# Expert passes cut at multiples of 128 of the running row count, summed into 64 on-chip slots and scattered from there without gaps

## The reference, cut to what matters

```python
# x: 4096 tokens x 128; E = 32 experts, K = 4, inner width I = 96
scores = sigmoid(x @ gate_w.T)
_, topk_ids = top_k(scores + e_bias, K)
topk_w = take_along_axis(scores, topk_ids); topk_w /= sum(topk_w)
combine = zeros(T, E).at[arange(T), topk_ids].add(topk_w)
a = silu(x @ w1[e]) * (x @ w3[e]) * combine[:, e]      # for every expert e
out = sum over e of a @ w2[e]
x = x + gb * out
```

## Time and profile before

| | us |
|---|---|
| median of 3 runs (730.47, 730.84, 735.51) | 730.84 |
| the profiled execution | 729.48 |
| its span, first to last instruction | 727.0 |
| PE busy | 489.9 (67%) |
| DVE busy | 442.6 (61%) |
| POOL busy | 420.3 (58%) |
| ACT busy | 278.1 (38%) |

### The profile page before, as it was taken

The page is one execution under the profiler, slowest core; times in us unless marked ns, Lnnn a source line. Parts: engine busy times, 40 slices in busy tenths (PEclk is TensorE's granted clock), DMA queues, the critical chain, the costliest instruction groups (busy, mean ns, idle before and its releaser), DMA issues.

```text
span 727.0 us, 15153 instructions
## 1 busy us (share of the span) xinstructions
PE 489.9 (67%) x4424; PEld 381.2 (52%) x4425; DVE 442.6 (61%) x1317; ACT 278.1 (38%) x579; POOL 420.3 (58%) x636
## 2 busy tenths in 40 slices
PE   2568888888887767766666623168768767667157
PEld 0335555555555555655445522067767766567136
DVE  5876888888888754777787787035344343433127
ACT  0256777877877634332433322012222222112000
POOL 5565666666665000477766777607777777677710
PEclk9868999999999999787788755579998899989569
DMA  7993000000060050011111111135334443341178
GB/s 217 293 263 104 0 0 1 0 0 0 0 232 4 1 174 1 28 59 50 57 53 53 54 57 58 57 103 139 104 103 119 115 114 102 98 120 52 51 282 310
DMA packets 65243, 65.94 MB, mean 91 GB/s; under 512 B 8896, under 2 KB 56224, under 8 KB 65200
## 3 DMA queue, kind: packets, MB, share of 16 engines
q1 hardware_dynamic: 47472, 41.28, 19.5%
q0 software_dynamic: 9216, 19.94, 8.1%
q10 hardware_dynamic: 8512, 4.20, 2.0%
HBM read 40.86 MB, written 27.67 MB: 94 GB/s over the span
## 4 chain that ended last, share of the span: by engine, by line
issue 25%; POOL 22%; DVE 20%; PE 19%; ACT 6%; DMA 4%; DVEq 2%; POOLq 1%; SPq 1%; ACTq 0%
POOL ys L630 16%; DVE L L1238 6%; PE PS L996 4%; POOL xs L617 4%; PE PS L881 2%; PE PS L1155 2%; PE PS L1008 2%; POOL QKR L515 1%; ACT YT L684 1%; PE PS L1019 1%; PE PS L856 1%; DMA srep<-in_scale 1%; PE PS L904 1%; PE PS L884 1%; DVE XH L1201 1%
## 5 line engine op out<-in xcount | busy, mean ns | idle before, releaser
L617 POOL DMA_INDIRECT xs<-QKT,posi x128 | 124.8, 975 | 109.3 <-issue 98.3
L1238 DVE TENSOR_TENSOR L<-PS,BIAS 128x768 f32<-128x768 f32 x128 | 116.6, 953 | 39.4 <-PE PS L884 33.7
L677 ACT ACTIVATE PR<-L 128x768 f32<-128x768 f32 x128 | 105.9, 842 | 60.9 <-DVE L L1238 58.7
L630 POOL DMA_INDIRECT ys<-hid,yidx x80 | 76.6, 958 | 45.7 <-issue 25.6
L1086 PE MATMUL PS<-BIAS,V 128*128 x320 | 68.0, 361 | 49.1 <-DVE V L1594 48.8
L630 POOL DMA_INDIRECT ys<-YT,yidx x80 | 76.6, 957 | 24.4 <-issue 23.2
L1086 PEld LDWEIGHTS PS<-BIAS,V 128*128 128x128 f32 x320 | 56.2, 205 | 55.5 <-issue 55.5
L791 ACT ACTIVATE L<-PS 128x384 f32<-128x384 f32 x40 | 19.6, 491 | 162.4 <-PE PS L1086 162.4
L881 PE MATMUL PS<-QKT 32*128 32x256 f32 x512 | 47.3, 439 | 27.2 <-DVE L L1238 25.7
L996 PE MATMUL PS<-YT,w1s 128*128 128x256 f32 x128 | 42.2, 487 | 15.8 <-ACT YT L741 15.8
L1608 DVE TENSOR_TENSOR hid<-PS,tag 128x512 f32<-128x512 f32 x20 | 13.8, 692 | 60.1 <-DMA ys<-hid,yidx 60.1
(11 more groups left out here) (247 smaller groups left out, 1121.4 us busy)
## 6 DMA issues: line engine op xcount, KB each, us to landing
PR<-xs SPq DMA_DIRECT2D x160, 72.0 KB
BIAS<-ys SPq DMA_DIRECT2D x12, 512.0 KB, 7.8
modb<-mod_rows SPq DMA_DIRECT2D x1, 4096.0 KB, 14.3
dist_rep<-dist_row SPq DMA_DIRECT2D x4, 768.0 KB, 7.1
xs<-pad_row SPq DMA_DIRECT2D x1, 2376.0 KB, 19.3
X<-in_x ACTq DMA_DIRECT2D x4, 512.0 KB, 6.9
BIAS<-dist_rep SPq DMA_DIRECT2D x4, 512.0 KB, 9.0
xs<-QKT,posi POOLq DMA_INDIRECT x128, 2.3
```

The source lines that it names most:

```text
L617: pool.indirect_dma_start(out=xs, out_offset=bass.IndirectOffsetOnAxis(ap=posi[j][:, t * TOPK + k:t * TOPK + k + 1], axis=0), in_=ROWS[j][ ...
L630: pool.indirect_dma_start(out=ys, out_offset=bass.IndirectOffsetOnAxis(ap=yidx[par][:, j:j + 1], axis=0), in_=yo[par][:, j * P:(j + 1) * P ...
L677: act.activation(PR[u % 4][:, :], L[u % 2][:, :], ACT.Exp).then_inc(s["exp_done"], 1)
L1238: return dve.tensor_tensor(L[u % 2][:, :].rearrange("p (j w) -> p j w", j=2), PS[:, at:at + 2, 0:HW], BIAS[:, u, :].rearrange("p (j w) -> ...
```

## The change

An expert's rows are still contiguous in its own region of `xs`. Now the rows of all experts, laid end to end, are also cut into 128 **slots** of 128 rows, at multiples of 128 of the running count. A pass is the part of one slot that belongs to one expert: it reads the 128 rows of `xs` that stand where the slot stands for that expert, which may begin before the expert's first row or run over its last. There it meets pad rows with weight 0 and place 0. The results of all passes of a slot are added, so each slot ends up full of real rows. For the counts given above that makes 159 passes; 160 are run, as before.

- **xs.** Pad rows are wanted in front of each region's first row (the 128 rows at the end of the region before it), and behind each expert's last row. The second kind depends on the count: SyncE waits for `pad_ready`, loads the 32 row numbers from `pads` and issues 32 DMAs of 128 rows; the loads of `xg` then wait for `pad_done` besides `scat`. GpSimd's wait for `zero_done` ahead of its first scatter goes.
- **Tables.** DVE computes the slot of each pass and, for each group of 4 slots, the number of passes after which the group is full (`tv` columns 4 to 6, `treg` rows 4 to 6). `skip`, `twice` and `slot_no` go.
- **Slots.** 64 slots lie side by side in `YQ`, a tile of 8,704 columns that takes the place of `Y` and `QKT`. There are 128 slots, so each place lives twice (`LIVES`). ScalarE clears four places of `YQ` and of `yidx` per step, two steps ahead (`clear`, 32 in all); for a second life it first waits on `yst` until the scatters of the first have landed.
- **VectorE.** `y_evac` loads the 4 slot numbers, then for each pass does one fused multiply and add of [128 x 128] from PSUM into the slot and one add of [128 x 1] into `yidx`. Before each it waits for the pass before it on its own semaphore. `y_ev` now counts passes, not steps. The wait for the scatters (`yst`) is no longer here.
- **ScalarE.** The copy of the transposed rows to `xgT` moves here from VectorE (L828 of the changed kernel). Its 40 steps are written out instead of looped.
- **GpSimd.** 128 scatters in groups of 4. Ahead of each group it loads the count of passes from `treg` and waits for `y_ev` to reach it.

```diff
+            sp.wait_ge(s["zero_done"], 32)
+            sp.wait_ge(s["pad_ready"], 1)
+            for g in range(NE // 8):
+                for row in load_many(mybir.EngineType.SP, pads, g * 8, DUMMY):
+                    sp.dma_start(xs[bass.ds(row, P), :], pad_row[:, :]).then_inc(s["pad_done"], 16)
...
             for i in range(GROUP):
                 sp.wait_ge(s[f"scat{i}"], 16 * NT * TOPK // GROUP)
+            sp.wait_ge(s["pad_done"], 16 * NE)
...
-            def y_rows(i, par):
-                pool.wait_ge(s["y_ev"], i + 1 + 2)
-                settle(pool)
-                for j in range(XG):
-                    pool.indirect_dma_start(
-                        out=ys, out_offset=bass.IndirectOffsetOnAxis(ap=yidx[par][:, j:j + 1], axis=0),
-                        in_=yo[par][:, j * P:(j + 1) * P], in_offset=None).then_inc(s[f"yst{par}"], 16)
-
-            with pool.Fori(0, XSTEPS // 2) as two:
-                y_rows(two * 2, 0)
-                y_rows(two * 2 + 1, 1)
+            def y_rows(life):
+                for half in range(2):
+                    groups = SLOTS // YGROUP // 2
+                    for q in range(groups):
+                        m = life * (2 * groups) + half * groups + q
+                        ends_at = pool.value_load(passes_of[:, bass.ds(m, 1)], min_val=1, max_val=XG * (XSTEPS + 2))
+                        pool.wait_ge(s["y_ev"], ends_at)
+                        settle(pool)
+                        for j in range(YGROUP):
+                            n = (half * groups + q) * YGROUP + j
+                            pool.indirect_dma_start(
+                                out=ys, out_offset=bass.IndirectOffsetOnAxis(ap=yidx[:, n:n + 1], axis=0),
+                                in_=YQ[:, n * D:(n + 1) * D], in_offset=None).then_inc(s[f"yst{n // 16}"], 16)
...
+            def rows_ev(i, par):
+                act.wait_ge(s["xt_pe"], i + 1)
+                act.activation(xgT[par], bank(par), ACT.Copy).then_inc(s["xg_ev"], 1)
+
+            def clear(n):
+
+                if n < SLOTS // XG * LIVES:
+                    m = n * XG % SLOTS
+                    if n == NT // XG:
+                        for j in range(GROUP):
+                            act.wait_ge(s[f"scat{j}"], 16 * NT * TOPK // GROUP)
+                    if n >= SLOTS // XG and m % 16 == 0:
+                        act.wait_ge(s[f"yst{m // 16}"], 16 * 16)
+                    act.activation(YQ[:, m * D:(m + XG) * D], zero[:, :].to_broadcast([P, XG * D]), ACT.Copy)
+                    act.activation(yidx[:, m:m + XG].bitcast(F32), zero[:, :].to_broadcast([P, XG]), ACT.Copy
+                                   ).then_inc(s["yz"], 1)
...
-            def y_evac(i, par, buf, turns=None):
+            def y_evac(i, par, buf):
+                slots = load_many(mybir.EngineType.DVE, slots_of, i * XG, SLOTS, XG)
                 dve.wait_ge(s["y_pe"], i + 1 + 2)
-                if turns is not None:
-                    dve.wait_ge(s[f"yst{par}"], turns * (16 * XG))
-                dve.tensor_tensor(yo[par].rearrange("p (j d) -> p j d", j=XG),
-                                  bank(6 + par).rearrange("p (j d) -> p j d", j=XG),
-                                  tag[buf][:, :, 0:1].to_broadcast([P, XG, D]), ALU.mult)
-                dve.tensor_tensor(yidx[par][:, :], tag[buf][:, :, 1], twice[:, bass.ds(i * XG, XG)], ALU.max
-                                  ).then_inc(s["y_ev"], 1)
+                dve.wait_ge(s["yz"], i + 1)
+                for k in range(XG):
+                    dve.wait_ge(s["y_ev"], i * XG + (2 * XG + k))
+                    settle(dve)
+                    to = YQ[:, bass.ds(slots[k] * D, D)]
+                    dve.scalar_tensor_tensor(to, bank(6 + par, D, k * D), tag[buf][:, k, 0:1], to, ALU.mult, ALU.add)
+                    at_ = yidx[:, bass.ds(slots[k], 1)]
+                    dve.tensor_tensor(at_, at_, tag[buf][:, k, 1:2], ALU.add).then_inc(s["y_ev"], 1)
```

More of the change, by code:

```diff
@@ L47 @@
 XG = 4
+SLOTS = 64
+LIVES = YROWS // (SLOTS * P)
+YGROUP = 4
 XSTEPS = XTILES // XG
@@ L193, in build @@
         place_no = sb("place_no", [P, NT * TOPK])
-        pad_no = sb("pad_no", [P, 1])
+        group_no = sb("group_no", [P, 2])
         cnt = sb("cnt", [P, NE])
-        cnti = sb("cnti", [P, NE], I32)
-        ntile = sb("ntile", [P, NE])
+        pads = sb("pads", [1, NE], I32)
+        ends = sb("ends", [P, NE])
+        endi = sb("endi", [P, 2, NE], I32)
+        edge = sb("edge", [P, 2, NE])
+        part = sb("part", [P, NE])
+        upto = sb("upto", [P, NE])
+        lead = sb("lead", [P, NE])
         tend = sb("tend", [P, NE])
@@ L800, in _, with step @@
             act.sem_inc(s["at_act"], 2)
[L802 to L806, removed]
-            silu(0, 0)
[L808 to L812, removed]
+            def rows_ev(i, par):
[12 more added lines that the diff above has]
+                                   ).then_inc(s["yz"], 1)
+                elif n < XSTEPS:
+                    act.sem_inc(s["yz"], 1)
+            def step(i):
+                if i + 1 < XSTEPS:
+                    silu(i + 1, (i + 1) % 2)
+                if i + 2 < XSTEPS:
+                    rows_ev(i + 2, i % 2)
+                a_T(i, i % 2)
+                clear(i + 2)
+            act.wait_ge(s["z_done"], NB + 1)
+            clear(0)
+            clear(1)
+            rows_ev(0, 0)
+            rows_ev(1, 1)
+            silu(0, 0)
+            for i in range(XSTEPS):
+                step(i)
             outv = out.rearrange("b (t p) d -> p (b t) d", p=P)
@@ L1065, in _ @@
             last.then_inc(s["tv_pe"], 1)
-            for j in range(2):
-                last = pe.matmul(bank(0, P, j * P), skip[:, j:j + 1].to_broadcast([P, P]), ident[:, :], start=True, stop=True)
+            pe.wait_ge(s["tv_ready"], 2)
+            for j in range(3):
+                last = pe.matmul(PS[0:1, 0, j * P:(j + 1) * P], tv[:, 4 + j:5 + j], ident[:, :], start=True, stop=True)
             last.then_inc(s["tw_pe"], 1)
@@ L1564, in _ @@
-            for j in range(2):
-                last = dve.scalar_tensor_tensor(last_at[:, j, :], iota_e[:, :], tv[:, j:j + 1], over[:, :],
-                                                ALU.is_equal, ALU.mult)
-            st(last)
+            st(dve.tensor_reduce(nt2[:, 0:2], gl[:, :, :], AX_X, ALU.add))
+            st(dve.tensor_scalar(tv[:, 0:2], tv[:, 0:2], float(NE - 1), None, ALU.min))
             st.wait()
-            st(dve.tensor_tensor(nt2[:, 0:2], tile_no[:, :], tv[:, 2:4], ALU.subtract))
@@ L1578, in _ @@
+            st(dve.tensor_reduce(rk[:, 2:3], gt[:, :], AX_X, ALU.add))
             st.wait()
-            dve.tensor_scalar(tv[:, 0:2], tv[:, 0:2], float(NE - 1), None, ALU.min).then_inc(s["tv_ready"], 1)
+            st(dve.tensor_scalar(wsum[:, :], wsum[:, :], float(YROWS // P), None, ALU.min))
+            st(dve.tensor_tensor(tv[:, 6:7], rk[:, 2:3], group_no[:, 1:2], ALU.add))
+            st.wait()
+            st(dve.tensor_scalar(late[:, :], wsum[:, :], float(SLOTS), float(-SLOTS), ALU.is_ge, ALU.mult))
```

134 lines of the change are left out of this document (75 added, 59 removed).

## The result

The changed kernel takes 690.67 us in the median of four runs (688.46 to 694.51), the kernel before 733.17 beside it (730.47 to 736.19): ratio 0.9425, 95% interval 0.9361 to 0.9489. It was measured twice more, each time beside new runs of the kernel before: 689.26 to 730.57 (0.9431, 0.9399 to 0.9464) and 689.12 to 730.64 (0.9427, 0.9404 to 0.9450). The forecast was 692.7, range 688 to 714.

A forecast was written before the change was run, and what follows sets the result against it. GpSimd's scatters were taken as the bound: 32 fewer at 1.263 us, less later-start costs, move the last scatter 38.1 us earlier. Profiled 729.5 - 38.1 = 691.4, with the median 1.4 above: 692.7 us, range 688 to 714.

The forecast's parts named there:

- The bound: Expert stage: GpSimd's gapless row of scatters at 1.263 us each sets the time; 32 fewer give -40.4 us.
- The wait that looked largest: VectorE's result copy in the expert loop waited 60.1 and 54.3 us for earlier scatters to `ys` to land.
- VectorE's pass: Expert loop: 0.26 + 0.15 + 0.14 = 0.55 us a pass, four 2.2, VectorE's whole step 3.5 us.
- The slower rival: Expert loop: VectorE's additions wait on each other, pass 1.21, step 6.1, total 772 us; slower from pass 0.94; chance 0.05.
- TensorE's step: Expert loop: 3.33/0.93 + 0.38 = 3.96 us; passes hold the last scatters only if a step is over 4.06 us.
- GpSimd's register load: Ahead of each scatter group: 0.505 + 0.193 us, hidden because the sequencer runs about 3 us ahead, so 0.
- The rival at 714: GpSimd's register loads are exposed, each group 5.75 instead of 5.05 us, 21.7 us in all; chance 0.08.
- The pads: SyncE's 32 DMAs ahead of the `xs` loads: 1 us for the last pads landing late, ends 0 to 5.
- The rival of a late start: Pads land 5 to 10 us behind the last scatter to `xs`: 698 to 703 us; chance 0.06.
- The start of the scatters: First scatters to `ys`: +1.5 us for four passes, +1 for pads; group 0 at 493.2, group 1 at 499.5.
- The clear: ScalarE's clearing of slots: 0.58 us and 0.2 for the small one, hidden; its wait for first-life scatters does not hold.
- The rule on VectorE's copies: Two-port VectorE copies block GpSimd's DMA descriptors; rival: 40 tag copies of 0.18 hold scatters, 7.2 us, total 700; chance 0.03.

The follow-up runs named there:

- at 815: Level of some groups of runs, in which the kernel before took 815.41, 815.3 and 820.4 us in the median instead of 730.

## Why the prediction was right

**The bound.** The reasoning went from the earlier trace rows: 160 scatters at 1.263 with nothing else in the row. It held to the end. 32 scatters were to give 40.4 us; the interval from first load to last scatter fell by 40.2, and giving the 32 back cost 40.4.

**The wait that looked largest.** 60.1 and 54.3 us of VectorE were read as a symptom of GpSimd's pace and given no value of their own. The kernel with 160 scatters in the changed form has no such wait on VectorE (ScalarE's clearing waits 20.4 us for scatters there), and its ratio is 0.9996: taking the wait off VectorE gave nothing.

**VectorE's pass** was mis-sized: 0.55 predicted, 0.66 measured. The products and the addition came as costed. The term that was off is the wait on its own result, 0.24 instead of 0.14. Four passes of 0.66 are 2.64 us, plus 0.55 and 0.17 for the product and the tags and a register load of 0.34: 3.70 us end to end, where VectorE's chain took 3.32 from start to start and the forecast said 3.5. An operation starts before the one ahead of it ends (the tags 0.46 behind a product of 0.55), and the load runs in the sequencer beside them; the sum was made as if neither held. So the 3.5 came out near the 3.32 by luck: a wait put too small and overlaps left out. The slower rival needed a pass of 0.94 and is far.

**TensorE's step** was the margin that worried me, 3.96 us against a limit of 4.06. It was 3.36, in the mean 3.42, so the margin was over 0.6 us a step and not 0.1. Two terms failed, both to the good side. The clock was taken as 0.93, from a stage in which TensorE kept waiting; without those waits it was granted 1.00 from 490 to 620 us. The kernel with 32 more scatters, which holds TensorE back again, shows both: from 480 to 520 us TensorE was busy 38.77 of 40 us at a granted clock of 0.97, from 540 to 600 busy 41.90 of 60 at 0.85. And 0.38 us of waiting for the copy of the transposed rows went away. Before, this wait was, in us in total, times, longest:

```profile
PE PS L1086 <- DVE V L1594: 48.8, 31, 3.7
```

In the changed trace TensorE waits for no such copy; ScalarE makes it right behind its silu. With the copy back on VectorE (at 815) the wait is there again, 32.7 us in 15 times. 3.33 us, the busy time of the earlier trace rows at clock 1.00 without either term, would have been the better forecast. That both terms erred to the good side was luck: by the prediction's own sum, 0.1 us a step to the other side and the passes would have set the end.

**GpSimd's register load** was put at nothing because its sequencer ran 3 us ahead. The loads were there and took 0.29 us, with register work of 0.15; by source line, ns min/median/max:

```profile
L648 POOLq FUSED_REGOPS  x62: 46/152/168, 465.6 to 640.1; - x62
L648 POOLq TENSOR_LOAD <-treg x32: 285/292/331, 465.2 to 639.8; - x32
```

The last load is at 639.8, some 15 us ahead of the scatter that it serves. The pitch at a group's border is 1.26 like all others, and it is so with a load ahead of every scatter too. The rival at 714 is out.

**The pads** were given 1 us and took 0: 32 DMAs at a pitch of 0.59, their register loads in it (0.57 and four loads were expected), over by 476.3, 2 us ahead of the first load. The rival of a late start is out.

**The start of the scatters** was put 2.5 us later, 1.5 for the longer chain and 1 for the pads. From first load to first scatter it is 19.84 us against 18.56: +1.3. The gap ahead of the second group was forecast at 1.2 and is 0.51, since step 2 came sooner.

**ScalarE.** The clear took 0.62 (0.58 estimated) and its small one 0.20 (0.2); it waited 0.6 us once for scatters of a slot's first life. The wait was forecast not to hold at all. It cost nothing at the end, as the prediction said of that case.

**The sum.** -38.1 forecast. Counted from the last scatter to `xs`, the last one to `ys` came 692.9 - 469.61 = 223.3 us later before and comes 658.93 - 475.72 = 183.2 later now: -40.1. Of the 2.0 us between, 1.2 are the start, the pads in it, and 0.7 the gap ahead of the second group. The tail from the last scatter's start to the end of the span is 33.7 us against 34.1. Taken off medians of the kernel before of 730.6 to 733.2, these 40.1 and the 0.4 of the tail give 690.1 to 692.7; measured were 689.1 to 690.7. So the medians fell by 41.3 to 42.5, 1 to 2 us more than the span explains. 0.6 of that lies outside the span (729.48 - 727.0 before, 694.51 - 692.6 now); the rest is not explained and no larger than the spread of the runs.

**The rule on VectorE's copies.** Scatters took 952 to 964 ns at a pitch of 1.262 us, with 40 tag copies beside them, from SBUF to SBUF in float32. The Trainium skill, page "SBUF — State Buffer", section "SBUF: two separate sides", would have let such a copy hold GpSimd's descriptors. No scatter here is longer, or later, by the 0.17 us of a copy; for copies of this size the trace does not show the rule. That rival is out.

## What to carry to other kernels

When one engine issues one kind of instruction in a gapless row, count its instructions: a change there is worth the pitch times the number, and the largest entry among the waits may only be that engine's pace seen from elsewhere. Before trusting a gain of that kind, work out from which step time on the other engines would take over, for every wait on a count; here the sum gave 4.06 us (no run tests it), and a measured 3.42 left room. A clock read in a stage that waits is no forecast of the clock once the waits are gone.

## What the hardware showed that I had not expected

TensorE's granted clock rose from a mean of 0.93 to 1.00 when its waits went, although it did the same products. When VectorE waits on a semaphore for its own last result, as ahead of each pass here, it stands idle for 0.24 us nearly every time (31.1 us over 122 waits), where the chain of the earlier trace rows had 0.14; what makes the difference is not shown. The load of a register took 0.34 us on VectorE and 0.29 on GpSimd, well under the single ones seen before. On GpSimd it hid completely behind queued work. On VectorE the first pass of a step stood 0.40 to 0.50 us idle behind the tags, so part of it may show there. And the same kernel took 862 us on one occasion and 729.5 on another, with the silus and the scatters as long as ever and over 100 us of unexplained standstills on ScalarE that the other trace lacks. Ratios then differ too (1.05 against 1.00), so two kernels are only compared beside each other and at one level.
